# Attention scores as three split products, weights normalised by a factor for each partition, keys turned a batch ahead

## The reference, cut to what matters

```python
kv_r = _apply_rope(kv_c, sin_k[None], cos_k[None])          # (64, 257, 128)
scores = jnp.einsum('bhsr,bhlr->bhsl', q_r, k_r)            # 16 heads, 32 queries, 257 keys
attn = jax.nn.softmax(scores, axis=-1)
ctx_c = jnp.einsum('bhsl,bld->bhsd', attn, kv_r)
ctx_lat = jnp.einsum('bhsd,hkd->bhsk', ctx_c, w_kc_kv)
return ctx_lat.transpose(0, 2, 1, 3).reshape(Bv, Sv, H * K) @ Wo.T
```

## Time and profile before

| what | us |
|---|---|
| median of 3 runs | 1603.76 |
| the profiled execution | 1603.56 |
| its span, first to last instruction | 1601.4 |
| TensorE matmuls busy | 1485.5 (93% of the span) |
| VectorE busy | 1139.9 (71%) |
| ScalarE busy | 811.1 (51%) |
| GpSimd busy | 541.8 (34%) |

### The profile page before, as it was taken

How to read it: one execution, slowest core, us unless ns; L and a number is a source line. 1 busy time by engine, 2 the same in 40 slices (tenths; PEclk the granted TensorE clock), 3 DMA queues, 4 the chain that set the end, 5 groups by cost and what they waited for, 6 DMA issues and landing times. The chain is left out here.

```text
span 1601.4 us, 26509 instructions
## 1 busy us (share of the span) xinstructions
PE 1485.5 (93%) x8136; PEld 1123.1 (70%) x8136; DVE 1139.9 (71%) x1820; ACT 811.1 (51%) x1739; POOL 541.8 (34%) x594
## 2 busy tenths in 40 slices
PE   4799999999978999999999977999898899999997
PEld 3577777777746777777777766888443478787876
DVE  6888777887648788788788853777687735556466
ACT  4566565666545555555555543555211355554554
POOL 4244333442025554544545513221351202222021
PEclk9899999999989999999999988999898899999999
DMA  4223334243565444544544514000244100000000
GB/s 152 68 81 111 105 110 119 75 122 95 182 219 126 119 119 105 125 111 106 129 107 108 139 21 172 0 0 0 84 174 158 45 1 1 27 1 26 0 27 27
DMA packets 140917, 140.05 MB, mean 87 GB/s; under 512 B 84150, under 2 KB 111926, under 8 KB 139708
## 3 DMA queue, kind: packets, MB, share of 16 engines
q1 hardware_dynamic: 140284, 138.54, 30.0%
q10 hardware_dynamic: 576, 0.81, 0.2%
HBM read 109.88 MB, written 27.39 MB: 86 GB/s over the span
## 5 line engine op out<-in xcount | busy, mean ns | idle before, releaser
L997 ACT ACTIVATE c_e<-c_sc_ps,c_peak 128x257 f32<-128x257 f32 x256 | 119.6, 473 | 219.4 <-DVE c_peak L900 219.4
L878 POOL TENSOR_TENSOR c_mixed_low<-c_whole,c_mixed_high 128x512 fp32r<-128x512 f32 x64 | 81.9, 1279 | 211.0 <-ACT c_mixed_high L1017 211.0
L77 DVE TENSOR_TENSOR b_rot_parts_low<-b_rot,b_rot_parts_high 128x1536 fp32r<-128x1536 f32 x64 | 136.0, 2125 | 21.9 <-ACT b_rot_parts_high L541 21.9
L278 POOL TENSOR_TENSOR b_turned_raw<-b_turn_part 128x384 f32<-128x384 f32 x32 | 70.1, 2190 | 166.2 <-DVE b_key_parts_low L77 165.0
L1571 PE MATMUL f_ps<-f_right,f_left 128*128 128x512 f32 x256 | 115.7, 613 | 8.4 <-ACT f_raw L1614 6.1
L70 PE MATMUL c_out_ps<-c_shared_high,c_mixed_high 128*128 128x512 f32 x256 | 112.2, 438 | 11.1 <-issue 10.1
L324 DVE TENSOR_TENSOR b_rot<-b_w_qr,b_angle 128x1536 f32<-128x1536 f32 x64 | 119.2, 1862 | 0.2
L70 PE MATMUL b_ps<-c_shared_high,b_wq_parts_high 128*128 128x512 f32 x256 | 108.5, 424 | 6.5 <-DVE c_shared_low L77 6.5
L70 PE MATMUL e_mm_ps<-folded_high,e_h_t_high 128*128 128x512 f32 x256 | 106.4, 416 | 5.7 <-DVE e_h_t_low L77 5.6
L541 ACT ACTIVATE b_rot_parts_high<-b_rot 128x1536 fp32r<-128x1536 f32 x64 | 95.3, 1489 | 24.5 <-PE b_ps L72 17.0
L274 POOL TENSOR_TENSOR b_turn_part<-b_early,b_centre 128x384 f32<-128x384 f32 x64 | 82.1, 1303 | 72.2 <-DMA b_early<-early 70.5
(11 more groups left out here) (232 smaller groups left out, 3903.8 us busy)
## 6 DMA issues: line engine op xcount, KB each, us to landing
c_ends_spread<-end_weights SPq DMA_DIRECT2D x64, 256.0 KB, 4.3
carried_queries<-x SPq DMA_DIRECT2D x7, 2048.0 KB, 11.3
b_early<-early SPq DMA_DIRECT2D x15, 640.0 KB, 4.0
f_left<-ent_in SPq DMA_DIRECT2D x16, 512.0 KB, 5.4
f_right<-ent_out SPq DMA_DIRECT2D x16, 512.0 KB, 6.5
c_q_first<-carried_queries SPq DMA_DIRECT2D x32, 224.0 KB, 3.3
c_q<-carried_queries SPq DMA_DIRECT2D x32, 224.0 KB, 3.2
b_late<-late SPq DMA_DIRECT2D x16, 320.0 KB, 3.8
```

Of the source, the lines that this page charges most:

```text
L77: return nc.vector.tensor_tensor(low, value, high.bitcast(F32), ALU.subtract)
L878: nc.gpsimd.tensor_tensor(mixed[1][:, w, :, u], whole[:, u % 2].rearrange("p (h s) -> p h s", h=H), mixed[0][:, w, :, u].bitcast(F32), ALU ...
L997: last = nc.scalar.activation(e[:, v, c], sc_ps[:, 2 * v + c, 0:L], ACT.Exp, bias=peak[:, v, c:c + 1], accum_out=total[:, v, c:c + 1])
```

## The change

- The scores become three fp32r products of 258 columns (`multiply_parts`), of queries and keys split into a high part (rounded by ScalarE) and a low part (subtracted by GpSimd). Queries and keys of batch b + 2 are rounded in the steps of batch b. The keys get a 258th, zero column.
- `normalise` scales by a factor for each partition: two `tensor_scalar` instructions of 257 columns take the place of the one `tensor_tensor`, the last key's column included.
- `keep_ends` goes from GpSimd to VectorE, as a copy of two elements per partition, right behind `find_peak`.
- The keys of batch b + 1 are turned and rounded in half 1 of batch b, and `split_kv(b)` stands right behind `keep_ends` in half 0, ahead of `normalise`.
- Only two buffers for the raw cache are left; the SyncE queue stores the last weights first, then loads the cache, spreads the last weights and loads the queries.
- The first two batches' last queries come by DMA, not from ScalarE. The holo weights' angles after the loop are reduced in three pieces, not two. Moments are kept at j = 6, squares taken at j = 4.

```diff
+            sp.wait_ge(qc_stored, 8 * HPAIRS)
+            crossing.staged_queries(sp, staged)
...
-                    if isinstance(U, int) and U >= 2 * HPAIRS - 2:
-                        at = (H - 2 + ab) * S + base
-                        nc.scalar.activation(crossing.q[:, :, at:at + G], ps[:, QC_BANK + ab].rearrange("p (b s) -> p b s", b=B)[:, 0:2], ACT.Copy)
...
             def tile(i, w):
                 for u in range(BT):
                     b = BT * i + u
-                    if known(i, 1):
-                        wait(sp, rotated_, b - BT + 1)
-                        crossing.load(sp, b, u)
...
+                    if known(i, 1):
+                        store_ends(i - 1, u)
+                    wait(sp, rotated_, b - 1)
+                    crossing.load(sp, b, u % 2)
                     if known(i, 1):
                         spread_ends(i - 1, u)
+                    wait(sp, scored, 2 * (b - BT) + 2)
...
-            def keep_ends(n, i, u, half):
-                pool.wait_ge(normed, n + 1)
-                v = u % 2
-                if half == 0:
-                    wait(pool, ends_stored[v], 32 * i + 16 * (u // 2))
-                nc.gpsimd.tensor_tensor(ends[:, v, 2 * half:2 * half + 2], e[:, half, :, END], inverse[:, half], ALU.mult).then_inc(ended, 1)
...
+            def split_queries(b, u):
+                pool.wait_ge(q_rounded, b + 1)
+                nc.gpsimd.tensor_tensor(q[u], q[u].bitcast(F32), q_high[:, u % 2].bitcast(F32), ALU.subtract).then_inc(q_split, 1)
+
+            def split_keys(b, u):
+                pool.wait_ge(key_rounded, b + 1)
+                nc.gpsimd.tensor_tensor(keys[1][:, u % 2], kv_even[u], keys[0][:, u % 2].bitcast(F32), ALU.subtract).then_inc(key_split, 1)
...
                 for j in range(STEPS):
-                    n, u, half = STEPS * i + j, j // 2, j % 2
+                    u, half = j // 2, j % 2
                     b = BT * i + u
-                    keep_ends(n, i, u, half)
+                    if half == 0 and not (isinstance(b, int) and (b == 0 or b + 1 >= B)):
+                        split_keys(b + 1, (u + 1) % BT)
                     if half == 0 and not (isinstance(b, int) and b + 2 >= B):
                         rotate(b + 2, (u + 2) % BT, i + (u + 2) // BT)
+                    if half == 1 and not (isinstance(b, int) and b + 2 >= B):
+                        split_queries(b + 2, (u + 2) % BT)
                     if half == 1 and (u or known(i, 1)):
                         split_mixed(b - 1, (u - 1) % BT, w if u else 1 - w)
...
                 nc.vector.reciprocal(inverse[:, v], total[:, v]).then_inc(dve_chained, 1)
                 dve.wait_ge(dve_chained, n + 1)
-                nc.vector.tensor_tensor(e[:, v, :, 0:END], e[:, v, :, 0:END], inverse[:, v].unsqueeze(2).to_broadcast([P, 2, END]), ALU.mult).then_inc(normed, 1)
+                for c in range(2):
+                    last = nc.vector.tensor_scalar(e[:, v, c], e[:, v, c], inverse[:, v, c:c + 1], None, ALU.mult)
+                last.then_inc(normed, 1)
+
+            def keep_ends(n, i, u, half):
+                v = u % 2
+                if half == 0:
+                    wait(dve, ends_stored[v], 32 * i + 16 * (u // 2))
+                dve.wait_ge(normed, n + 1)
+                nc.vector.tensor_copy(ends[:, v, 2 * half:2 * half + 2], e[:, half, :, END]).then_inc(ended, 1)
...
                     if more:
                         find_peak(n + 1, 1 - half)
+                    keep_ends(n, i, u, half)
+                    if half == 0:
+                        split_kv(b, u)
                     if half == 1 and (u or known(i, 1)):
                         add_end(i - (u == 0), (u - 1) % BT)
                     if more:
                         normalise(n + 1, 1 - half)
                     split_turned(n, u, half)
-                    if half == 0:
-                        split_kv(b, u)
...
+            parts = [(phase[:, 0:D], flat(crossing.raw_pair)[:, 0:D]), (phase[:, D:2 * D], flat(crossing.swapped_pair)[:, 0:D]),
+                     (phase[:, 2 * D:], flat(table[:])[:, 0:HOLO - 2 * D])]
...
+            def round_queries(b, u, t):
+                act.wait_ge(q_loaded[u], queries_in(u, t))
+                wait(act, scored, 2 * b - 2)
+                nc.scalar.activation(q_high[:, u % 2], q[u].bitcast(F32), ACT.Copy).then_inc(q_rounded, 1)
+
+            def round_keys(b, u):
+                act.wait_ge(rotated_, b + 1)
+                wait(act, scored, 2 * b - 2)
+                nc.scalar.activation(keys[0][:, u % 2], kv_even[u], ACT.Copy).then_inc(key_rounded, 1)
...
                     round_turned(n, b, u, half)
-                    if half == 0:
-                        round_kv(b, u)
+                    if half == 1 and not (isinstance(b, int) and b + 1 >= B):
+                        round_kv(b + 1, (u + 1) % BT)
                     if half == 1 and (u or known(i, 1)):
                         round_mixed(b - 1, (u - 1) % BT, i if u else i - 1, w if u else 1 - w)
+                    if not (isinstance(b, int) and b + 2 >= B):
+                        if half == 0:
+                            round_queries(b + 2, (u + 2) % BT, i + (u + 2) // BT)
+                        else:
+                            round_keys(b + 2, (u + 2) % BT)
...
+            round_keys(0, 0)
+            round_queries(0, 0, 0)
             exponential(0, 0)
+            round_kv(0, 0)
+            round_keys(1, 1)
+            round_queries(1, 1, 0)
...
                 if half == 0:
-                    pe.wait_ge(q_loaded[u], queries_in(u, t))
-                    pe.wait_ge(rotated_, b + 1)
+                    pe.wait_ge(q_split, b + 1)
+                    pe.wait_ge(key_split, b + 1)
                 wait(pe, exped, n - 1)
                 for c in range(2):
                     at = slice((2 * half + c) * P, (2 * half + c + 1) * P)
-                    last = nc.tensor.matmul(sc_ps[:, 2 * half + c, 0:L], q[u][:, at], kv_t[u], start=True, stop=True)
+                    last = multiply_parts(nc, sc_ps[:, 2 * half + c, 0:LE], [q_high[:, u % 2, at], q[u][:, at]], [a[:, u % 2] for a in keys], True, True)
...
                     turn_weights(n, half)
-                    if half == 0:
-                        turn_kv(b, u)
+                    if half == 1 and not (isinstance(b, int) and b + 1 >= B):
+                        turn_kv(b + 1, (u + 1) % BT)
```

More of the change, by code:

```diff
@@ L730, in rotate_first @@
         nc.gpsimd.tensor_tensor(part[:, 1], self.swapped[0], self.table[:, 1], ALU.mult).then_inc(self.pool_chained, 1)
+        nc.gpsimd.memset(self.keys[:, L:], 0.0).then_inc(self.padded, 1)
         pool.wait_ge(self.pool_chained, 2)
-        nc.gpsimd.tensor_tensor(self.keys[:], part[:, 0], part[:, 1], ALU.add).then_inc(self.rotated, 1)
+        pool.wait_ge(self.padded, 1)
+        nc.gpsimd.tensor_tensor(self.keys[:, 0:L], part[:, 0], part[:, 1], ALU.add).then_inc(self.rotated, 1)
     def first(self, sp):
@@ L752, in cross_attention @@
         END = L - 1
-        raw_later, swapped_later = sb("c_raw_later", [P, BT - 2, L]), sb("c_swapped_later", [P, BT - 2, L])
-        crossing.raw += [raw_later[:, u] for u in range(BT - 2)]
-        crossing.swapped += [swapped_later[:, u] for u in range(BT - 2)]
         table, raw, swapped = crossing.table, crossing.raw, crossing.swapped
         table_loaded, raw_loaded = crossing.table_loaded, crossing.raw_loaded
-        part = sb("c_part", [P, 2, L])
-        kv_later = sb("c_kv_t", [P, BT - 1, L])
-        kv_t = [crossing.keys[:]] + [kv_later[:, u] for u in range(BT - 1)]
+        part = spare[:, 0:2 * L].rearrange("p (n l) -> p n l", n=2)
+        LE = L + 1
+        kv_later = sb("c_kv_t", [P, BT - 1, LE])
+        kv_even = [crossing.keys[:]] + [kv_later[:, u] for u in range(BT - 1)]
+        kv_t = [a[:, 0:L] for a in kv_even]
         kv = pair("c_kv", [P, BT, 2, P])
-        q_later = sb("c_q", [P, BT - 2, H * S])
+        q_later = sb("c_q", [P, BT - 2, H * S], F32R)
         q = [crossing.q[:, u] for u in range(2)] + [q_later[:, u] for u in range(BT - 2)]
+        q_high = sb("c_q_high", [P, 2, H * S], F32R)
+        keys = pair("c_key", [P, 2, LE])
         peak = sb("c_peak", [P, 2, 2])
@@ L798, in queries_in @@
         def queries_in(u, t):
-            return 32 * t + (16 if u < 2 else 32)
+            return 32 * (t + 1)
         def in_tiles(engine, tile):
@@ L817, in _, with store_ends @@
         def _(sp):
+            def store_ends(i, u):
+                b, v = BT * i + u, u % 2
+                sp.wait_ge(ended, 2 * b + 2)
+                sp.dma_start(ends_dram[bass.ds(b, 1)].rearrange("b p c -> p (b c)"), ends[:, v]).then_inc(ends_stored[v], 16)
             def spread_ends(i, u):
@@ L844, in tile @@
                              x_tiles[bass.ds(i, 1)].rearrange("t p d -> p (t d)")).then_inc(x_loaded, 16)
-            for u in range(2, BT):
-                crossing.load(sp, u, u)
```

(7 more changed lines are left out.)

53 lines of the change are left out of this document (30 added, 23 removed).

## The result

The changed kernel takes 1633.1 us (median of four runs, 1632.3 to 1634.4) where the kernel before took 1603.6 beside it: ratio 1.0181, interval 1.0168 to 1.0194. Slower by 1.8%; the prediction was 1620, with 1634 as the upper end of its range.

A forecast was written before the change was run, and what follows sets the result against it. VectorE's ring was taken to bound, slightly longer than TensorE's. Tile 0 +2.4, tile 1 +1.2, tiles 2 to 14 +7.8, tile 15 +0.5, start 4.4, end 0.5: +16.8 on 1603.56, forecast 1620, range 1590 to 1634.

The forecast's parts named there:

- Queued behind them nothing waits. Cost nothing: SyncE's queue: caches and queries issued 1.5 us later, last weights 0.5 later, over 1.8 us left before each is read.
- the 0.5 given: Tile 15, the last of the loop: predicted to take 0.5 us more than before.
- one column a cycle, with the copy held: Rival: VectorE's scalings of 257 columns run at one column a cycle and the copy is held; 1634 us, chance 0.05.
- Scores: TensorE: six 258-column products at 0.127 us, 0.76 for 0.86 a step; 0.8 us a tile, counting only where TensorE paces.
- The rival of the weight loads: TensorE: 0.19 us weight loads no longer hidden under 258-column products; 31.2 us a tile, 1628 us, chance 0.08.
- Normalising and its exclusion: VectorE: scalings of 0.35 us, 0.63 a pair, 0.07 less than now; GpSimd instructions can hold scalings and the two-element copy.
- The ring's sum: VectorE's chain from peak to peak, with GpSimd's holds laid out by hand: four batches sum to 30.4 us a tile, against 29.8.
- copy not held: Rival: GpSimd holds VectorE's scalings but not its two-element copy; 7.10 us a batch, 29.5 a tile, 1606 us, chance 0.18.
- two rings near each other: Kernel before: TensorE's work sums to 28.0 of a tile's 29.8 us, and VectorE's ring is slightly the longer.
- The gain of the keys turned earlier: Half 0: `split_kv` moves from the ring's tail into the 1.09 us gap before the reciprocal; up to 0.6 us a batch.
- Start: Before the first peak: two more DMAs, then rounding, low part and products; peak at 467.3 for 462.87, 4.4 us, bounds 3 and 7.
- What would show it: Signs: scalings 0.35 by median, many 0.5 to 1.0; half 1 copies 0.5 or more; tiles near 30.4; first peak 4 us later.

The follow-up runs named there:

- products_alone: Changed kernel with normalising, keeping of the last key's weights and turning of the keys as in the kernel before, and SyncE's end in mended order: 1604.55 us, ratio 1.0005.
- two_copies: Changed kernel with VectorE's copy of two elements per partition made as two copies of one: 1622.8 us, ratio 1.0121.
- short_queries: Changed kernel with SyncE's end mended and GpSimd's low part of the queries made for 2 of 512 columns: 1613.0 us, ratio 1.0070.
- two_copies_and_end: Changed kernel with copies of one element, and tile 15's first two batches' last weights stored and spread ahead of the holo loads: 1615.1 us, ratio 1.0081.

## Why the prediction came out as it did

- **The mis-sized step is SyncE's.** The prediction said of the reordered queue "Queued behind them nothing waits. Cost nothing". Inside the loop that held: from tile 0 to the end of the stage `add_end` waited 10.2 us in all for its spread weights, 8.9 of them at once in tile 15. There it failed, since behind the loop a new wait for the last rotation and five loads stand ahead of the first store, and I had costed only the queue inside the loop. 11.4 us for the 0.5 given; the other terms sum to 18.8 for 16.3. With the queue mended the time is 1624.8, near the forecast of 1620. That 1633.1 still lies inside the range, by 0.9 us, is luck: the upper end is the time of a rival that the rows refute (one column a cycle, with the copy held), and no bound of the prediction was about the end of the queue.
- **Scores.** 0.127 us a product was predicted, 0.119 measured; 0.15 us a step gained on TensorE, which shows whole in `products_alone` (3.39 to 3.23 in half 1). The rival of the weight loads (1628) is refuted: loads of 0.19 us follow each other at 0.119.
- **Normalising and its exclusion.** The scalings' 0.35 and 0.63 a pair hold. Who is held, and by whom, was right in half 1 (the copy held for 0.68 by hand, for 0.83 in tile 9's batch: 0.99 in place of 0.16) and in half 0 (the first scaling behind both products, the second ahead of the sum; the first took 0.85 us for 0.58 by hand).
- **The ring's sum was right, its claim of a sole cause was not.** A tile of 30.4 was forecast and 30.4 found. Cut as the forecast cuts them, half 0 first, tile 9's batches are 7.54, 7.51, 7.78 and 7.51 for the forecast 7.42, 7.60, 8.05 and 7.32 (the last reaches into tile 10): errors of 0.1 to 0.3 us that cancel. And the rival "copy not held" gave 29.5 a tile, where `two_copies` and `short_queries` show 29.9: behind the copy stood TensorE's step of 3.88 in half 1. I had summed TensorE by tile (28.0 of 29.8, "two rings near each other") and never by step, so I put the move of `turn_kv` on no path. Of the 3.0 us a tile that VectorE gets back with the copy's hold, 0.5 show.
- **The gain of the keys turned earlier**, "up to 0.6 us a batch", is 0.08 alone (29.8 to 29.5 a tile) and 0.14 with the transposes in the wait.
- **Start** 5.4 for 4.4: the table load comes 1.2 us later (461.83 for 460.60). The queries are there, and rounded, from 464.55, where the forecast had 463.4; from there the chain runs as laid out (split at 465.25, peak at 468.27: 3.7 us for 3.9). Kernels that are the same up to there had the first peak at 467.6 (`two_copies_and_end`) to 470.2 (`two_copies`), so the term is 4.7 to 7.4.
- **Tiles 0 and 1** were given 2.4 and 1.2 and took 0.9 and 2.0. The granted clock in tile 0 was 0.76, before 0.89; what that costs there isn't separated.
- **What would show it**: median near 0.35 (0.356) with many held, ends 0.15 us behind GpSimd's, long copies, the gap gone in half 1, tiles at 30.4, the first peak some 4 us later all came. TensorE isn't waited for by `find_peak` in the changed kernel (0.3 us in 11 tiles). That line too says only which of two equal rings is last, not by how much.

## What to carry to other kernels

Sum every engine by step, not by stage, and ask of a moved instruction on which side of its engine's wait it lands: in the kernel before, the keys a batch ahead were worth 0.3% with their transposes behind the wait and 0.7% with them ahead of it; in the changed kernel the same move gained next to nothing, while the held instructions grew by about what it freed. When the order of a queue in a loop changes, read its epilogue as well, for that is where a wait that the loop hides comes ahead of a store that everything needs. Where two engines exclude each other, an edit that shifts their phase has a price that none of its instructions has by itself, so try parts together and not only one by one.

## What the runs showed of the hardware

- VectorE's copy of one element per partition was never held by GpSimd (256 copies in `two_copies_and_end`, 0.147 us at most), and its copy of two elements was (1.252 at most). Other instructions of one element weren't tried. The Trainium skill (SBUF — State Buffer, section "Who interferes with whom") has the loser of the shared ports blocked for the other's whole instruction; the trace agrees, with the copy due at 741.12 ending at 742.11, 0.03 us behind GpSimd's instruction of 740.78 to 742.08. No row of before had shown a two-element copy.
- fp32r products of 258 columns follow each other at 0.119 us by the median in tiles 2 to 12 (granted clock 1.00) and at 0.215 in front of the first peak (0.50, that is 1.2 GHz). At 1.00 the weight loads, 0.19 us each, are hidden under them.
- A store to DRAM of the last weights took 4.7 us until its spread could be issued when five larger loads had been issued just before it, and 1.4 when none had.
- Behind an interval of 12.0 us in which TensorE was busy for 3.1, the granted clock was 0.63 for the next 5.5 us and then 1.00 again (957.8 to 961.3).
- Kernels that are alike up to the stage's first peak had it at 467.6 (`two_copies_and_end`) to 470.2 us (`two_copies`), in one profile each: 2.6 us of start, over half of the 4.8 us that the prediction took as what a comparison can tell.
